# Two graph layers on one core: groups that begin with one tile, degree masks shared by two engines, a rebuilt last stage

## The reference

```python
# layer 0: graph convolution with self loops
deg  = segment_sum(w, dst) + 1
norm = rsqrt(deg)[src] * w * rsqrt(deg)[dst]
out0 = relu(segment_sum((x @ W0)[src] * norm, dst) + self_term + b0)
x1   = layernorm(x + out0)
# layer 1: tensor messages; idx_i = src, idx_j = dst
xs, xv = x1[:, :128] @ Win_s, einsum(x1[:, 128:] as 128x3, Win_v)
Wf   = (shifted_softplus(rbf @ Wf1 + bf1) @ Wf2 + bf2) * edge_weight
m    = products of xs[dst], xv[dst], the direction of r_ij, and Wf
agg  = segment_sum(m, src)
S    = shifted_softplus(agg_scalars @ W1_s) @ W2_s
V    = agg_vectors @ W1_v @ W2_v
out  = layernorm(x1 + concat(S, V))
```

## Time and profile before

| | |
|---|---|
| median of 3 runs | 1092.49 us |
| lowest and highest | 1091.48 and 1096.86 us |
| the profiled execution | 1102.86 us |
| its span, first to last instruction | 1101.1 us |
| busy: TensorE, VectorE, ScalarE, GpSimd | 84%, 78%, 64%, 54% |

### The profile page before, as it was taken

The page is one execution under the profiler, slowest core; times in us unless marked ns, Lnnn a source line. Parts: engine busy times, 40 slices in busy tenths (PEclk is TensorE's granted clock), DMA queues, the critical chain, the costliest instruction groups (busy, mean ns, idle before and its releaser), DMA issues.

```text
span 1101.1 us, 17479 instructions
## 1 busy us (share of the span) xinstructions
PE 925.9 (84%) x4812; PEld 747.4 (68%) x4812; DVE 856.4 (78%) x2617; ACT 701.0 (64%) x1617; POOL 592.4 (54%) x679
## 2 busy tenths in 40 slices
PE   4989888989973999999999289999999999625553
PEld 4958777767753888888888168788788878514442
DVE  5888888868724788888879278888888888529997
ACT  0068877777761576676666346666666666439998
POOL 4017888788851566675666426677677765310000
PEclk9999999989995999999999699999999999955555
DMA  9979999999998599999997758999999998587996
GB/s 354 419 227 223 251 238 238 233 233 238 231 217 283 178 339 322 326 331 316 318 338 247 268 157 184 222 210 206 218 222 200 216 222 166 75 229 292 381 378 249
DMA packets 121553, 280.66 MB, mean 255 GB/s; under 512 B 13746, under 2 KB 38342, under 8 KB 121462
## 3 DMA queue, kind: packets, MB, share of 16 engines
q1 hardware_dynamic: 73590, 186.31, 46.8%
q0 software_dynamic: 35392, 82.86, 39.6%
q10 hardware_dynamic: 12480, 10.42, 2.9%
HBM read 132.44 MB, written 147.10 MB: 254 GB/s over the span
## 4 chain that ended last, share of the span: by engine, by line
PE 47%; ACT 8%; DMA 5%; issue 5%; DVE 3%; POOL 1%; SPq 0%; ACTq 0%; POOLq 0%; DVEq 0%
PE bank L1237 11%; PE bank L1284 6%; PE bank L1268 6%; PE bank L1241 5%; PE bank L1298 5%; PE bank L1296 3%; PE bank L1228 3%; PE bank L1262 2%; PE bank L1294 2%; PE bank L1269 2%; DMA edge_mem<-x 1%; ACT node_mem L799 1%; ACT node_mem L781 1%; ACT node_mem L791 1%; ACT edge_mem L770 1%
## 5 line engine op out<-in xcount | busy, mean ns | idle before, releaser
L532 POOL DMA_INDIRECT sum<-R_mem,sidx_all x79 | 128.6, 1628 | 93.9 <-DVE sidx_all L923 52.6
L589 POOL DMA_INDIRECT sum<-R_mem,l_sidx x79 | 130.3, 1650 | 52.9 <-ACT R_mem L727 18.2
L581 POOL DMA_INDIRECT G_mem<-x_d,dst_i x79 | 86.8, 1099 | 87.7 <-PE bank L1273 65.0
L1237 PE MATMUL bank<-G_hi 128*128 128x512 f32 x316 | 132.0, 418 | 0.0
L1237 PE MATMUL bank<-G_lo,G_hi 128*128 128x512 f32 x316 | 125.3, 396 | 0.0
L1153 PE MATMUL bank<-G_hi,M_mem 128*128 128x512 f32 x200 | 87.3, 437 | 9.9 <-ACT R_mem L630 9.9
L1314 PE MATMUL bank<-ident,node_mem 128*128 128x128 f32 x80 | 27.5, 447 | 71.4 <-DVE node_mem L1088 71.4
L1241 PE MATMUL bank<-G_hi,G_lo 128*128 128x512 f32 x316 | 85.5, 392 | 0.0
L1268 PE MATMUL bank<-edge_mem,Winv 128*128 128x512 f32 x158 | 82.6, 605 | 0.0
L1029 DVE SCALAR_TENSOR_TENSOR edge_mem<-edge_mem,Y,bank 128x128 f32<-128x128 f32 x237 | 71.3, 386 | 14.2 <-ACT edge_mem L733 14.2
L1153 PE MATMUL bank<-G_lo,M_mem 128*128 128x512 f32 x200 | 81.1, 406 | 0.0
(11 more groups left out here) (213 smaller groups left out, 2921.6 us busy)
## 6 DMA issues: line engine op xcount, KB each, us to landing
filt_d<-node_mem SPq DMA_DIRECT2D x40, 512.0 KB
node_mem<-filt_d SPq DMA_DIRECT2D x79, 256.0 KB
node_mem<-sum SPq DMA_DIRECT2D x39, 512.0 KB, 6.0
sum<-zeros SPq DMA_DIRECT2D x33, 512.0 KB
G_mem<-x SPq DMA_DIRECT2D x20, 512.0 KB, 6.6
x_d<-node_mem SPq DMA_DIRECT2D x20, 512.0 KB, 3.6
edge_mem<-x SPq DMA_DIRECT2D x19, 512.0 KB, 6.3
x_d<-R_mem SPq DMA_DIRECT2D x19, 512.0 KB, 3.7
```

The lines of the kernel that those rows point to most:

```text
L532: pool.indirect_dma_start(sum0, bass.IndirectOffsetOnAxis(ap=sidx[:, t:t + 1], axis=0), R[t % 8][:, :], None, compute_op=ALU.add).then_inc ...
L581: pool.indirect_dma_start(G3[t % 8][:, :], None, x1_d, bass.IndirectOffsetOnAxis(ap=dst_i[:, t:t + 1], axis=0)) \
L589: pool.indirect_dma_start(sum1, bass.IndirectOffsetOnAxis(ap=l1_sidx[:, t:t + 1], axis=0), R3[t % 8][:, :], None, compute_op=ALU.add).then ...
L1237: pe.matmul(bank[4 + a][:, :], zT_hi[a][:, c * P:(c + 1) * P], w[c][:, :], start=(c == 0 and w is W0h), stop=False)
```

## The change

1. **Degrees.** The two hardware loops are written out. From tile 14 on, ScalarE makes `hot_lo` of every even tile with two activations, relu(1 - |part - iota|); VectorE makes the rest. The two prepared weights move into the loop, behind tile 50. `inverse_root` moves ahead of the first step of the next stage.
2. **Groups of three** of layer 1 now are tile 0 alone, then 1 to 3, 4 to 6, up to 76 to 78. In the second step `counts1` moves behind `sidx`.
3. **Filters** are written to and read from `filt_d` in pairs, each partition one 4 KB run.
4. **End of the node stage.** The roots of the last three tiles are made by VectorE; the last tile is normalised there too. `sum1` stores get their own semaphores, those of the last two pairs are queued behind the last `x1_d` store, and the gathers of layer 1 wait for `x1_d` alone up to tile 8.
5. **Edges of layer 1.** Rings of twelve for gathered rows and for sums. `Wins` moves behind the transpose into bank 5. `msg_hi`, `msg_lo`, the mask and the sums come one step sooner. Scatters follow gathers by six groups and not five.
6. **Last stage.** The root's arithmetic goes to GpSimd; the softplus is max(x, 0) + ln(0.5 exp(-|x|) + 0.5), so that VectorE does one operation and not two; the second normalisation of a pair moves from ScalarE to VectorE. 14 buffers in turn.

```diff
+def by_act(t):
+    return t >= 14 and t % 2 == 0
+def first(g):
+    return max(3 * g - 2, 0)
 def tiles_of(g):
-    return min(3 * g + 3, TR) - 3 * g
+    return first(g + 1) - first(g)
...
+def filter_pair(dram, i):
+    return dram[i * 256:(i + 1) * 256, :].rearrange("(p k) d -> p (k d)", k=2)
...
@@ scalar, degrees
+            for t in range(T):
+                if by_act(t):
+                    tmp = spare[t // 2 % 2]
+                    act.wait_ge(s_deg_mm, t - 2)
+                    st.mark(act.activation(tmp, iota_f[:, :], ACT.Abs, bias=part[:, 0, t:t + 1], scale=-1.0))
+                    st.settle(act)
+                    st.mark(act.activation(hot_lo[t % 4], tmp, ACT.Relu, bias=1.0, scale=-1.0))
+                if t == MIDWAY:
+                    w_prep()
...
@@ vector, degrees
+            for t in range(T):
                 wait(dve, s_deg_mm, t - 2)
-            skewed(dve, hots, 0, 4)
+                if not by_act(t):
+                    dve.tensor_scalar(hot_lo[t % 4][:, :], iota_f[:, 0:P], part[:, 0, t:t + 1], None, ALU.is_equal).then_inc(s_deg_hot, 1)
...
+            inverse_root()
             for s in range(T4 + 1):
...
-                    inverse_root()
...
-                        counts1()
                     dve.wait_ge(e_dup, 4 * (g + 1))
...
+                    if s == 1:
+                        counts1()
...
@@ gpsimd, start of layer 1
             for u in range(8):
-                pool.wait_ge(n_st[u], 32 * (T2 // 8))
-            pool.wait_ge(s_zero1, 16 * (T2 + 4))
-            pool.wait_ge(w_sidx, 2)
+                pool.wait_ge(n_st[u], 16 * (T2 // 8))
...
+                        if t == 8:
+                            pool.wait_ge(n_keep, TR)
+                            for u in range(8):
+                                pool.wait_ge(rows_st[u], SUM1)
...
-                if g >= 5:
-                    r = g - 5
+                if g >= 6:
+                    r = g - 6
                     if r:
-                        pool.wait_ge(f_scat, 48 * r)
+                        pool.wait_ge(f_scat, 16 * first(r))
...
@@ gpsimd, last stage
+            for t in range(T2):
+                a = t % 4
+                w, st = tiny4[a], Stage(g_rstd, t, K_ROOT)
+                pool.wait_ge(g_mv, K_MV4 * (t + 1))
+                st.mark(pool.tensor_scalar(w[:, 0, :], mv4[a][:, :, 1], EPS, None, ALU.add))
+                st.mark(pool.tensor_scalar(w[:, 7, :], mv4[a][:, :, 0], -1.0, None, ALU.mult))
+                pool.wait_ge(g_rs, 2 * (t + 1))
...
@@ vector, end of the node stage (per group g of the last two)
+                dve.tensor_scalar(w[:, 0, :], mv[a][:, :, 1], EPS, None, ALU.add)
+                dve.wait_ge(n_rs, 2 * (g + 1))
+                st.mark(dve.scalar_tensor_tensor(w[:, 3, :], w[:, 2, :], -0.5, w[:, 2, :], ALU.mult, ALU.mult))
...
+            dve.tensor_scalar(r, r, w[:, 5, 0:1], w[:, 6, 0:1], ALU.mult, ALU.add).then_inc(n_last, 1)
...
@@ tensor, edges of layer 1
-                    pe.matmul(bank[3][:, 0:P], Wins[:, :], rawT[b][:, 512:640], start=True, stop=True).then_inc(f_wv, 1)
                 if live(s, 4):
...
                     pe.transpose(bank[5][:, 256:384], G3[a][:, 0:C], ident[:, :]).then_inc(f_tr, 1)
-                if live(s, 10):
+                if live(s, 5):
+                    pe.matmul(bank[3][:, 0:P], Wins[:, :], rawT[b][:, 512:640], start=True, stop=True).then_inc(f_wv, 1)
+                if live(s, 9):
...
@@ scalar, edges of layer 1
-                if live(s, 8):
-                    t, a = s - 8, u
+                if live(s, 7):
+                    t, a = s - 7, (u - 7) % 8
                     act.wait_ge(f_msg, K_MSG * (t + 1))
...
@@ scalar, last stage
-                if live(s, 7, T2):
-                    normalise(1)
                 if live(s, 0, T2):
                     st.settle(act)
-                    st.mark(act.activation(sx[u][:, 2, :, :], sx[u][:, 1, :, :], ACT.Ln, bias=1.0))
+                    st.mark(act.activation(sx[u][:, :, :], sx[u][:, :, :], ACT.Ln, bias=half_c[:, :], scale=0.5))
...
@@ vector, last stage
-                    dve.tensor_scalar(sr[u][:, :, :], al[s % NA][:, :, 0:C], 0.0, -LOG2, ALU.max, ALU.add).then_inc(g_sr, 1)
...
-                    dve.tensor_tensor(sp[a1][:, :, :], sr[a1][:, :, :], sx[a1][:, 2, :, :], ALU.add).then_inc(g_sp, 1)
...
+                    dve.scalar_tensor_tensor(sp[a1][:, :, :], al[t1 % NA][:, :, 0:C], 0.0, sx[a1][:, :, :],
+                                             ALU.max, ALU.add).then_inc(g_sp, 1)
+                if live(s, 7, T2):
+                    dve.wait_ge(g_rstd, K_ROOT * (t7 + 1))
+                    dve.tensor_scalar(al[b7][:, 1, :], al[b7][:, 1, :], tiny4[a7][:, 5, 1:2], tiny4[a7][:, 6, 1:2],
+                                      ALU.mult, ALU.add).then_inc(g_y1, 1)
```

More of the change, by code:

```diff
@@ L33, with place @@
 Y1 = float(np.sqrt(3.0 / (4.0 * np.pi)))
-def skewed(eng, step, tail, lead, unroll=4, steps=T):
-    for s in range(lead):
-        step(s, s % unroll)
-    with eng.Fori(lead // unroll, steps // unroll) as j:
-        for u in range(unroll):
-            step(j * unroll + u, u)
-    for s in range(steps, steps + tail):
-        step(s, s % unroll)
+def by_act(t):
+    return t >= 14 and t % 2 == 0
 def live(s, lag, steps=TR):
     return not isinstance(s, int) or 0 <= s - lag < steps
+def first(g):
+    return max(3 * g - 2, 0)
 def tiles_of(g):
-    return min(3 * g + 3, TR) - 3 * g
+    return first(g + 1) - first(g)
+def place(t):
+    g = (t + 2) // 3
+    return g, t - first(g)
 def extra(s):
@@ L63, in counted @@
 def counted(s):
-    return 3 * s + sum(tiles_of(extra(k)) for k in range(s) if extra(k))
-def turn(t, slot, n):
-    return t // n if isinstance(t, int) else (t - slot) // n
+    return first(s) + sum(tiles_of(extra(k)) for k in range(s) if extra(k))
 def wait(eng, sem, value):
@@ L336, in build @@
         f_filt = [sem(f"f_filt{i}") for i in range(4)]
-        f_gather = [sem(f"f_gather{i}") for i in range(8)]
+        f_gather = [sem(f"f_gather{i}") for i in range(12)]
         f_proj0 = sem("f_proj0")
@@ L364, in build @@
         g_rstd = sem("g_rstd")
-        g_y = sem("g_y")
-        g_st = [sem(f"g_st{i}") for i in range(8)]
-        hold = {e: sem(f"hold_{e}") for e in ("pool", "sync", "vector", "scalar")}
-        def held(eng, s, value):
-            if isinstance(value, int):
-                wait(eng, s, value)
-            else:
-                name = {nc.gpsimd: "pool", nc.sync: "sync", nc.scalar: "scalar", nc.vector: "vector"}[eng]
-                eng.wait_ge(s, value)
-                eng.sem_inc(hold[name], 1)
+        g_y0 = sem("g_y0")
+        g_y1 = sem("g_y1")
+        rows_st = [sem(f"rows_st{i}") for i in range(8)]
         NZ = 8
@@ L686, in nodes0, with root @@
                     act.activation(tiny[a][:, 1, :], mv[a][:, :, 1], ACT.Ln, bias=eps_c[:, :]).then_inc(n_rs, 1)
+                def root(g):
+                    a = g % 4
+                    act.wait_ge(n_rs, 2 * g + 1)
+                    act.activation(tiny[a][:, 2, :], tiny[a][:, 1, :], ACT.Exp, scale=-0.5).then_inc(n_rs, 1)
+                if tail:
+                    log((s - 9) // 2)
                 if live(s, 2):
@@ L698, in nodes0 @@
                 if tail:
-                    act.wait_ge(n_rs, 2 * g + 1)
-                    act.activation(tiny[a][:, 2, :], tiny[a][:, 1, :], ACT.Exp, scale=-0.5).then_inc(n_rs, 1)
+                    root((s - 9) // 2)
+                if s == LATE + 10:
+                    for g in (T2 - 2, T2 - 1):
+                        log(g)
+                        root(g)
                 if live(s, 5, TAIL):
@@ L719, in _ @@
                 nodes0(s, s % 8)
+            for u in range(8):
+                act.wait_ge(rows_st[u], SUM1)
             def edges1(s, u):
-                e = s - 11
+                e = s - 10
                 def sums_out(t):
                     act.wait_ge(f_mm, t + 1)
-                    wait(act, f_scat, 48 * (t // 3 - 1))
-                    act.copy(R3[t % 8][:, :], bank[sum_bank[t % 3]][:, :]).then_inc(f_ev, 1)
+                    if t >= NE:
+                        act.wait_ge(f_scat, 16 * first(place(t - NE)[0] + 1))
+                    act.copy(R3[t % NE][:, :], bank[sum_bank[place(t)[1]]][:, :]).then_inc(f_ev, 1)
                 if live(s, 7):
@@ L778, in nodes1 @@
+                    act.wait_ge(g_tr, t + 1)
+                    wait(act, g_mm, t - 3)
+                    act.copy(spT[a][:, :, :], bank[a][:, 0:256].rearrange("p (k c) -> p k c", k=2)).then_inc(g_spT, 1)
                 if live(s, 0, T2):
@@ L1280, in edges1 @@
                     for k in range(j + 1):
-                        if k == j:
-                            wait(pe, f_ev, 3 * g - 2 + k)
+                        if k == j and g and k < tiles_of(g - 1):
+                            pe.wait_ge(f_ev, first(g - 1) + k + 1)
                         for part_ in (msg_hi, msg_lo):
```

(2 more changed lines are left out.)

320 lines of the change are left out of this document (173 added, 147 removed).

## The result

The changed kernel takes 1075.91 us (median of 4 runs, 1073.80 to 1078.46), the kernel before, beside it, 1092.22. The ratio is 0.9843, with a 95% interval of 0.9805 to 0.9881. A second comparison on another occasion gave 0.9875 (0.9848 to 0.9902). So the change is worth some 14 to 17 us, less than the 27.3 that I forecast, and 1075.9 lies 10.7 us above the predicted time.

The account below looks back on a forecast made before the run. Bounds: TensorE (degree loop, layer 0 nodes, layer 1 edges), GpSimd (layer 0 edges), ScalarE (last stage). Savings 0.5 + 3.0 + 8 + 5.9 + 9.4 = 26.8, with pipeline start 27.3; 1092.5 - 27.3 = 1065.2 us, range 1060 to 1070, 8 in 10 1051 to 1078.

Parts of the forecast that it names:

- Masks on ScalarE, 0: Degree loop: ScalarE making some masks saves 0, because TensorE's beat stays; up to 7.2 us at the upper clock.
- The stalls: Degree loop: three VectorE stalls, 7.7 us, taken as staying; the rival that they go too gives 1057.5, chance 0.24.
- Weights and root, -0.5: End of degree loop: weights moved inside, inverse root ahead of the next stage; net 0.5 us less.
- the order of counts: Second step: `counts1` behind `sidx` makes the first scatter sooner, TensorE's next step waits longer; within the net -0.5.
- Nodes to edges, -3.0: Last node statistics to first layer 1 gather: store 1.8 us sooner, wait for `x1_d` alone 1.2; 3.0 us less.
- Layer 1, the order, -8: Layer 1 edges: `Wins` behind the transpose starts copy L742 sooner, closing a TensorE hole; 27 x 0.3 = 8.1, taken as 8.
- Layer 1, the end, -5.9: End of layer 1 edges: tile 78 scattered with its group, not alone after waiting for a landing; 5.9 us less.
- the shorter pipeline, -0.5: Added to the sum: half a microsecond less for the shorter start of the pipeline.
- Last stage, -9.4: Last stage: ScalarE loses a normalisation, VectorE becomes the bound; a pair takes 2.54 us, not 2.78, 39 x 0.24 = 9.4 less.
- Layer 0: Layer 0: edges stay bound by GpSimd issue, nodes by TensorE's matmuls; larger filter packets 0 to -2, taken as 0.
- The last stage stays: Rival: last stage stays at 2.78 us a pair, through DMA's limit or GpSimd holding up VectorE; 1074.6, chance 0.13.
- Written-out code starves: Rival: instruction fetches starve written-out code in the first 60 us, slower than before; 1102 with 14 stalls, chance 0.03.

Follow-up runs that it names:

- four variants of the changed kernel: Changed kernel with, in turn, second normalisation on ScalarE (1.0005), root on VectorE (1.0048), aggregation behind softplus (0.9847), old groups of three (0.9931); ratios to the kernel before.
- the first and third set: Follow-up runs of the changed kernel and its variants, each set on one chip beside the kernel before, which took 1091.4 and 1091.2 us.
- the later aggregation: Changed kernel with VectorE aggregating last-stage statistics behind residual sum and softplus of the next pairs; ratio to the kernel before 0.9847, again 0.9805 (1070.95 us).
- second profile of before: The kernel before, unchanged, profiled and timed once more; ratio 1.0007, span 1086.9 us.

## Why the prediction was right in direction and 10.7 us off

By the stages of the two profiles, 27.3 us were forecast and 14.4 came. Of the 12.9 that are missing 0.5 are at the start, 3.2 in layer 0, 1.8 between nodes and edges, 2.2 in layer 1 and 5.2 in the last stage. The time lies outside the forecast's own range (1060 to 1070) and inside the range for 8 in 10 (1051 to 1078), near its upper end. That end was drawn for rivals of which none came true, so it holds in part by luck.

**Masks on ScalarE, 0.** Right: same beat, same time without them.

**The stalls.** I took them as staying, as a cost of the loop or not, and gave 0.24 to their going. The weak step is another: "I take the saving as it is", from a profile 10.4 us slower than the median. The stalls were in the first profile of before and in four variants of the changed kernel, and where they are absent, as in the first and third set, the path at the start is another one. On it the clears decide. This step cost little: of the 14.2 us between the two profiles of before 13 lie ahead of the last statistics, where only 0.5 us of the sum was to be saved.

**Weights and root, -0.5, and the order of counts.** Measured 0 at the first scatter, and 0 to 3 us by the times. A move ahead of a wait that ends last elsewhere is worth nothing; the wait for the clears stood in no row of the first profile, because `sidx` came later.

**Nodes to edges, -3.0.** Measured 1.2. The step as far as the store is right: `x1_d` was issued 603.61 - 598.63 = 5.0 us behind the last statistics before and 3.2 after. What failed is that the landing was taken as fixed: it took 6.7 us from the second store's issue at about 605.1, where the `sum1` store of before, issued at 603.98, let the gather go at 609.65, 5.7 later. How long the last `x1_d` store took to land, before and after (DMA rows of the windows 602 to 610 and 603 to 612 us):

```profile
x_d<-R_mem SPq DMA_DIRECT2D x1, 256.0 KB, 3.7
```

```profile
x_d<-R_mem SPq DMA_DIRECT2D x1, 256.0 KB, 5.9
```

After, SP issues the last two pairs' stores together, and at 607.62, ahead of their landing, two filter loads of 512 KB, which before went out ahead of 593 us; the window after moved 3.70 MB, that before 2.15. That these bytes are the reason was not tested.

**Layer 1, the order, -8.** The mechanism is right, shown by its reversal; the size fails by a slip of the prediction. It starts the copy 0.22 us sooner and leaves 0.08 of the hole of 0.3, and then multiplies the 27 groups by 0.3 all the same; 27 x 0.22 is 5.9. The profiles have 0.21 to 0.22 us a group, some 5 to 6 us. The idle time of 0.50 of the earlier trace rows is 0.27 after, of which the prediction's usual gap is 0.2:

```profile
806.76 0.30 PEld L1357 LDWEIGHTS bank<-MV,edge_mem 128*128 128x128 f32 x2 [0.27 <-issue]
```

TensorE's run over all tiles went from 311.1 to 306.4 us.

**Layer 1, the end, -5.9, and the shorter pipeline, -0.5.** Together measured 7.8 (from TensorE's last transposes to the first load 36.6 us before, 28.8 after). The sum is near, its parts are not. The grouping alone is 2.4 and not 5.9: the prediction has the last group start where that of 75 to 77 did, and it starts 2.0 us later. The other 5.4 I read as the sums one step sooner, a step of 3.9 us that I had put at half a microsecond, and the last scatter of 16 rows, 1.2 us, which I had overlooked. (With the old groups, where that scatter lands alone, it is 2.9 us to the load, before 5.0.) The split of the 5.4 was not tested.

**Last stage, -9.4.** Measured 4.2: the largest error. The bound is VectorE, as forecast. The pace went from 2.78 us to 2.64 and not to 2.54, and two turns of the changed kernel's steady part take 2.9 to 3.0. The mis-sized term is the normalisation, 0.32 forecast and 0.46 measured: its nearest row had half the elements and took 0.17 from start to start, and doubling that is not enough. VectorE is busy 9.59 of 10 us, 2.53 of a pair, where 2.41 was forecast. Its waits, 0.11, are about the 0.13 that the forecast had left it; the 0.18 behind its own statistics could have been saved, as the later aggregation shows.

**Layer 0.** Forecast unchanged. It took 3.2 us longer in one profile and 7.0 in the other than in the second profile of before. Between fourth scatter and last statistics, however, the two profiles of before are 522.3 and 528.3 us, the changed kernel's 525.4 and 529.7, and its ten variants' 524.2 to 529.1. Whether the change costs anything here stays open; packet size was tried and gave no answer.

**The rivals.** "The last stage stays" gives 1074.6, nearest to the time, but neither of its reasons holds: the DMA engines carried 415 GB/s, and VectorE's price is the same without GpSimd. The nearness is luck. "Written-out code starves" is not seen on the chips without stalls. Whether the long step at the start of layer 1 on the other chip has to do with it is open.

## What to carry to other kernels

Where a profiled execution is slower than the timed median, find what in it is not in the median before a saving is subtracted: ask of each stall what would be waited for if it were gone. An engine's wait for its own last result is work that another instruction of the same engine can cover: moving the aggregation gained 7 us, the whole rebuild of the stage 4.2. Price an edit for every engine that it touches; new operand forms on ScalarE took a quarter of what the moved normalisation freed.

## What the runs showed of the hardware

- An activation with an addend read from memory took 0.09 us longer to the next start than one without (0.19 against 0.10, 0.40 against 0.31).
- A GpSimd operation beside VectorE's 512-element normalisation took 0.37 us and otherwise 0.19; the normalisation took 0.54 with GpSimd at work and with GpSimd idle.
- Loads and stores together ran at 415 GB/s with a DMA share of 1.03; 399 at 1.01 was no limit, though it looked full.
- On one chip the profiles of four variants, all written out, showed stalls of TensorE, VectorE and ScalarE at two places, beside GpSimd's gathers; the first profile of before had those of the degree part in a hardware loop. The kernel before took 8 us longer on that chip. The cause is open.
- In the first 55 us the granted clock reads 1.00, while TensorE's passes take what they take at 0.50 (four of 128x128 in 1.06 us).
